# Transposed adjacency parts made beside attention, column sums by matmul, and row statistics made in the last head

## The reference

```python
def _L0_gnn_ref(x, spatial_encoding, edge_encoding, Wq, Wk, Wv, Wout):
    ...
    q = (x @ Wq).reshape(h, n, d)
    k = (x @ Wk).reshape(h, n, d)
    v = (x @ Wv).reshape(h, n, d)
    a = jnp.einsum('hnd,hmd->hnm', q, k) * scale
    a = a + spatial_encoding + edge_encoding
    mask = spatial_encoding == 0.0
    a = jnp.where(mask, -1000000.0, a)
    a = jax.nn.softmax(a, axis=-1)
    a = jnp.where(mask, 0.0, a)
    out = jnp.einsum('hnm,hmd->hnd', a, v)
    out = out.transpose(1, 0, 2).reshape(n, h * d)
    return out @ Wout
def _L1_gnn_ref(X, S, W1, W2, W3, U1, U2, U3, gamma, beta):
    ...
    Rf = S / jnp.clip(S.sum(axis=1, keepdims=True), 1e-12)
    Rb = S / jnp.clip(S.sum(axis=0), 1e-12)[:, None]
    for s in range(STEPS):
        A = _adj_from_feats(Xa, W1, W2, W3)
        Xf = Rf @ Xf
        Xb = Rb @ Xb
        Xa = A @ Xa
        ...
h = jnp.maximum(_layernorm(x, axis=-1), 0.0)
x = x + _L0_gnn_ref(h, adj, adj, L0_gnn_Wq, L0_gnn_Wk, L0_gnn_Wv, L0_gnn_Wout)
h = jnp.maximum(_layernorm(x, axis=-1), 0.0)
x = x + _L1_gnn_ref(h, adj, L1_gnn_W1, ...)
```

## Time and profile before

| | us |
|---|---|
| median of 3 runs | 3375.74 (3369.71 to 3376.3) |
| the profiled execution | 3375.48 |
| its span, first to last instruction | 3373.6 |
| PE busy | 2892.8 (86%) |
| DVE busy | 2192.1 (65%) |
| ACT busy | 1342.0 (40%) |

### The profile page before, as it was taken

The page is one execution under the profiler, slowest core; times in us unless marked ns, Lnnn a source line. Parts: engine busy times, 40 slices in busy tenths (PEclk is TensorE's granted clock), DMA queues, the critical chain, the costliest instruction groups (busy, mean ns, idle before and its releaser), DMA issues. The chain is left out here.

```text
span 3373.6 us, 55939 instructions
## 1 busy us (share of the span) xinstructions
PE 2892.8 (86%) x20376; PEld 2147.8 (64%) x20376; DVE 2192.1 (65%) x4346; ACT 1342.0 (40%) x1734; POOL 59.8 (2%) x71
## 2 busy tenths in 40 slices
PE   2469999999999999999999778878884669687599
PEld 1356676766767667676676447656553556576488
DVE  7966555565555655556556488788488887895531
ACT  5743434434344343443434322333326364522221
POOL 0000000000000000000000000000000000000110
PEclk7579999999999999999999889998997889899899
DMA  7937848578485784857848413000010010100500
GB/s 288 371 144 178 195 107 199 124 177 196 106 199 124 177 196 105 199 124 177 197 102 210 120 47 98 26 13 26 26 38 26 1 51 2 50 26 1 231 1 26
DMA packets 587856, 396.80 MB, mean 118 GB/s; under 512 B 538563, under 2 KB 553414, under 8 KB 562118
## 3 DMA queue, kind: packets, MB, share of 16 engines
q1 hardware_dynamic: 585990, 382.49, 42.1%
q10 hardware_dynamic: 1728, 12.58, 1.1%
HBM read 223.05 MB, written 37.75 MB: 77 GB/s over the span
## 5 line engine op out<-in xcount | busy, mean ns | idle before, releaser
L773 DVE SCALAR_TENSOR_TENSOR e_lo<-e,e_hi 128x2048 f16<-128x2048 f32 x128 | 293.2, 2291 | 435.3 <-ACT e_hi L688 435.3
L625 PE MATMUL av<-vw_hi,pT_hi 128*128 128x256 f16 x2048 | 559.5, 273 | 8.0 <-DMA pT_lo<-e_lo 8.0
L625 PE MATMUL av<-vw_hi,pT_lo 128*128 128x256 f16 x2048 | 559.4, 273 | 0.0
L625 PE MATMUL av<-vw_lo,pT_hi 128*128 128x256 f16 x2048 | 559.4, 273 | 0.0
L614 PE MATMUL logits<-kT_hi,qT_hi 128*128 128x512 f16 x1024 | 388.6, 379 | 2.8 <-DVE att_small L759 1.9
L614 PE MATMUL logits<-kT_lo,qT_hi 128*128 128x512 f16 x1024 | 388.1, 379 | 0.0
L614 PE MATMUL logits<-kT_hi,qT_lo 128*128 128x512 f16 x1024 | 388.1, 379 | 0.0
L682 ACT ACTIVATE att_small<-att_small,minus 128x1 f32<-128x1 f32 x128 | 37.6, 294 | 784.3 <-DVE att_small L768 784.3
L759 DVE CUSTOM_DVE_ANT_0 e<-logits,bias,att_small 128x1024 f32<-128x1024 f32 x256 | 328.6, 1283 | 0.4 <-issue 0.3
L2000 DVE SCALAR_TENSOR_TENSOR nuc_junk<-nuc_e,nuc_thr 128x2048 bf16<-128x2048 f32 x140 | 323.7, 2348 | 4.3 <-issue 0.4
L683 ACT ACTIVATE e<-e,att_small,sc 128x2048 f32<-128x2048 f32 x128 | 266.2, 2080 | 0.0
(11 more groups left out here) (417 smaller groups left out, 5802.6 us busy)
## 6 DMA issues: line engine op xcount, KB each, us to landing
bias<-bias_scratch SPq DMA_DIRECT2D x130, 1024.0 KB, 4.9
bias_scratch<-adj_bias SPq DMA_DIRECT2D x16, 1024.0 KB, 4.5
adjT_scratch<-adjT SPq DMA_DIRECT2D x16, 1024.0 KB, 5.8
nuc_at_hi<-adjT_scratch SPq DMA_DIRECT2D x32, 512.0 KB, 3.8
nuc_at_lo<-adjT_scratch SPq DMA_DIRECT2D x32, 512.0 KB, 4.6
adjT<-adjT_scratch SPq DMA_DIRECT2D x16, 1024.0 KB, 19.8
adj_rows<-in_adj_dram ACTq DMA_DIRECT2D x12, 1024.0 KB, 6.8
adj_rows<-in_adj_dram SPq DMA_DIRECT2D x4, 1024.0 KB, 14.0
```

What stands on the lines that cost most here:

```text
L625: last = nc.tensor.matmul(AV[par], PT[par][w][:, m, :], VW[x][:, m, :], start=(m == 0 and w == x == 0), stop=(m == T - 1 and w == 1))
L773: nc.vector.scalar_tensor_tensor(out=EL[:, :], in0=E[par][:, :], scalar=P_SCALE, in1=EH[:, :], op0=ALU.mult, op1=ALU.subtract).then_inc(lo ...
```

## The change

**Adjacency.** The stage no longer transposes. It keeps the bias part. The column sums come from TensorE: a column of ones against each tile of rows, 4 f32 matmuls of 512 columns per tile, accumulated over the 16 tiles in PSUM; at the end ScalarE copies the row of sums, 16 small matmuls turn it, and VectorE copies it to `deg`.

**Pieces.** The transposed parts are made in `attend`, in heads 3 to 7, in 64 pieces of 128 rows x 512 columns. Their buffers are the columns of `hT_hi` and `hT_lo` that belong to heads 0 to 3. Slot n is the n-th of the 14 slots per head; in slot n SyncE loads piece n, ScalarE and VectorE make high part and remainder of piece n-1, SyncE issues two DMA transposes of piece n-2, and at the head of the slot four stores of piece n-3 in runs of 128 f16. The loops of heads 3 to 7 are written out.

**Projection banks.** K's eight batches go to eight different PSUM banks (`K_BANKS`) and not to two and then a ring of four. In head 0 ScalarE evicts VW ahead of the first `exp`, and `weight_tops` comes earlier on VectorE.

**Statistics.** `bn_stats` and `bn_aggr` of a row tile follow the last `add` of that tile in head 7; `refresh` reads them.

```diff
 def adjacency(...)
+                pe.wait_ge(ones_here, 1)
+                for n in range(T):
+                    pe.wait_ge(loaded[n % AHEAD], 16 * (n // AHEAD) + 16)
+                    for b in range(N // BANK):
+                        cols = slice(b * BANK, (b + 1) * BANK)
+                        last = nc.tensor.matmul(CS[0:1, cols], ones[:, 0:1], A[n % AHEAD][:, cols], start=n == 0, stop=n == T - 1)
+                    last.then_inc(summed, 1)
...
-                    s.wait_ge(at_stored[q], 16 * turn + 16)
-                    for h in range(2):
-                        s.wait_ge(tposed, 2 * n + h + 1)
-                        nc.scalar.activation(half(AT[q][:, 0, :, :], h), TP[q][:, HALF * h:HALF * (h + 1)], ACT.Copy,
-                                             scale=A_SCALE).then_inc(hi_done, 1)
...
+                        s.wait_ge(summed, AHEAD * i + u + 1)
...
-                            nc.vector.tensor_reduce(col[:, T // 2 * h:T // 2 * (h + 1), ds(n, 1)].rearrange("p m a -> p (m a)"),
-                                                    TP[q][:, HALF * h:HALF * (h + 1)].rearrange("p (m n) -> p m n", n=P), X, ALU.add)
...
 def attend(...)
+                def piece_load(n):
...
+                    if n >= 2:
+                        sp.wait_ge(piece_lo, n - 1)
+                    sp.dma_start(PA[n % 2], piece_rows[tile // 2, tile % 2, part, :, :]).then_inc(piece_here[n % 2], 16)
+                def piece_turns(n):
...
+                    sp.wait_ge(piece_lo, n + 1)
+                    if n:
+                        sp.wait_ge(piece_stored, 64 * n)
+                    for x in range(2):
+                        sp.dma_start_transpose(PX_T[x], PX[x]).then_inc(piece_turned, 16)
+                def piece_stores(n):
...
+                    sp.wait_ge(piece_turned, 32 * n + 32)
+                    for x in range(2):
+                        for q in range(2):
+                            sp.dma_start(piece_out[tile, part % 2, :, x, :, q, part // 2, :],
+                                         PX_T[x][q * HALF:(q + 1) * HALF, :, :]).then_inc(piece_stored, 16)
...
+                def items_and_pieces(h):
+                    for t in range(T):
+                        piece_stores(slots(h, t))
+                        item(T * h + t, (t + 2) % T, t % 2)
+                        piece_turns(slots(h, t))
+                        piece_load(slots(h, t))
...
+                def piece_top(n):
...
+                    s.wait_ge(piece_here[n % 2], 16 * (n // 2) + 16)
+                    if n:
+                        s.wait_ge(piece_turned, 32 * n)
+                    nc.scalar.activation(PX[0].rearrange("p (c r) -> p c r", c=CH), permuted(PA[n % 2]), ACT.Copy,
+                                         scale=A_SCALE).then_inc(piece_hi, 1)
+
+                def items_and_pieces(h):
+                    for t in range(SLOTS):
+                        exp(T * h + t + 2, t % 2)
+                        piece_top(slots(h, t))
...
+                def piece_rest(n):
...
+                    v.wait_ge(piece_hi, n + 1)
+                    nc.vector.scalar_tensor_tensor(out=PX[1].rearrange("p (c r) -> p c r", c=CH), in0=permuted(PA[n % 2]), scalar=A_SCALE,
+                                                   in1=PX[0].rearrange("p (c r) -> p c r", c=CH), op0=ALU.mult, op1=ALU.subtract).then_inc(piece_lo, 1)
...
+                    for t in range(SLOTS):
+                        item(h, t, t % 2, link)
+                        if h == HEADS - 1:
+                            shift(T * h + t, t, t % 2)
+                            statistics(T * h + t, t)
+                        piece_rest(slots(h, t))
```

More of the change, by code:

```diff
@@ L351, in _ @@
             @block.tensor
             def _(pe):
-                with pe.Fori(0, T // AHEAD) as i:
-                    for u in range(AHEAD):
-                        n, q = AHEAD * i + u, u % 2
-                        pe.wait_ge(loaded[u], 16 * i + 16)
-                        rows_u = permuted(A[u][:, :])
-                        for h in range(2):
-                            pe.wait_ge(lo_done, 2 * n + h + 1)
-                            for t in range(T // 2 * h, T // 2 * (h + 1)):
-                                last = nc.tensor.transpose(TP[q][:, t * P:(t + 1) * P], rows_u[:, t // 2, t % 2 * P:(t % 2 + 1) * P], ident[:, :])
-                            last.then_inc(tposed, 1)
@@ L367, in _ @@
+                pe.wait_ge(row_here, 1)
+                for t in range(T):
+                    last = nc.tensor.matmul(CT[:, t:t + 1], permuted(col[0:1, :])[:, t // 2, t % 2 * P:(t % 2 + 1) * P], ones[0:1, 0:1],
+                                            start=True, stop=True)
+                last.then_inc(turned, 1)
             @block.scalar
@@ L886, in _, with turn_of_heads @@
                 tops_apart()
-                with v.Fori(0, HEADS - 1) as h:
-                    link = items(h)
+                def turn_of_heads(h, link):
                     weights(h + 1)
@@ L902, in _ @@
                     masks(2, 0, link)
-                link = items(HEADS - 1, ends=True)
+                with v.Fori(0, FIRST_HEAD) as h:
+                    turn_of_heads(h, items(h))
+                for h in range(FIRST_HEAD, HEADS - 1):
+                    turn_of_heads(h, items_and_pieces(h))
+                link = items_and_pieces(HEADS - 1)
                 lo(T * HEADS - 1, 1, link)
@@ L1323, in refresh @@
         with block:
-            if norm:
+            if norm is not None:
                 @block.sync
@@ L1406, in _ @@
                 for b in range(QUADS + 2):
-                    if norm and b < QUADS:
+                    if norm is not None and b < QUADS:
                         s.wait_ge(centred, b + 1)
```

222 lines of the change are left out of this document (132 added, 90 removed).

## The result

| | us |
|---|---|
| before, median of 4 runs | 3372.72 (3365.39 to 3376.3) |
| after, median of 4 runs | 3785.53 (3780.88 to 3790.46) |
| ratio | 1.1226, 95% interval 1.1204 to 1.1248 |
| profiled span, before and after | 3373.6 and 3783.9, +410.3 |
| mean granted TensorE clock, before and after | 0.936 and 0.907 |

The changed kernel is 12.3% slower. The forecast was slower, 3665, in a range of 3470 to 3785: the direction and the place are right, the size is 120 us short, and the median lies just outside the range.

The account below looks back on a forecast made before the run. With pieces, SyncE's in-order queue was taken to bound attention. From 3375.5 us: adjacency -57, small parts -4, -3 and -0.5, attention +354 (+342 slots, +18 turns of heads, -6 catching up) gave 3665, range 3470 to 3785.

Parts of the forecast that it names:

- part 3: Attention, heads 3 to 7: the next `e_hi` waits for a closed path through SyncE's in-order queue; sum 16.3, taken as 16.2 us.
- Part 1: Adjacency stage, 141 us before: less work on VectorE and ScalarE, 16 MB less DMA; about -57 us, bounds -47 to -61.
- The floors of DMA and ScalarE: Adjacency stage: DMA done at 141 us at the earliest, ScalarE's floor at 138.
- DMA loses 16 MB of 46 ... 141 at the earliest: Adjacency stage: the remaining 29.4 MB at 372 GB/s take 79 us from about 62, so 141 at the earliest.
- Part 2: Attention loop: a piece's copy on ScalarE and remainder on VectorE lengthen the item from 10.53 to 12.4 us.
- the transpose behind the bias: SyncE's queue: the transpose of `e_hi` waits for the bias (lands 4.9 after issue), then needs 2.4 more; 7.0 us.
- Slots: Attention, heads 3 to 7: 60 slots pay the longer period, 60 x (16.2 - 10.5) = +342 us.
- The four turns of heads: Attention: ScalarE and VectorE come some 5.7 us later to K's first evictions; +4.5 us each, +18.
- Part 4: Small changes: K over eight banks -4 us, VW evicted before `exp` in head 0 -3, statistics moved -0.5.
- The statistics: Moved from the refresh's start into the last head: -0.5 us in the refresh, 0 in the head, 10 at the most.
- C: Rival: piece stores cost 0.93 us each on SyncE, period 18.1, time 3792; chance 0.08 given for it and D.
- D: Rival: TensorE's clock falls to 1.2 GHz in attention, bursts of 20.8 us bind, 3930; chance 0.08 given with C.

## Why the prediction was right or wrong

The mechanism of the forecast was right and its size was short. The step that failed is the sum in part 3, the closed path through SyncE: 16.3 us added up, 18.6 measured. Of the 120.8 us between forecast and measured change, attention has 115.1 (+462.1 where parts 2 to 4 gave +347), the adjacency stage 13.3 and the refresh 1.3; the nucleus takes 9.3 back, and the rest is 0.4.

**Part 1, -57, measured -43.7**, outside the bounds given (-47 to -61). The floors of DMA and ScalarE were about right, but they weren't what bound. The step that failed is "DMA loses 16 MB of 46 ... 141 at the earliest": the stores of the bias land 7.4 us after their issue (the page's median), there are two bias buffers, and VectorE waited for them 9 times, a term that the sum didn't have. With four the stage ends within 3 us of the forecast.

**Part 2, 12.4.** Measured alone 12.2 to 12.5, but by two errors that cancel. The remainder takes 1.08, the upper bound given ("up to 1.1 if the permuted read costs extra"), not 0.69; and the items of heads 3 to 7, written out, take 10.1 without a piece, not 10.53. The high part took 1.10 as said.

**Part 3, 16.2, measured 18.6.** The path was right in each of its steps and in their order. Term by term, forecast and mean of 54 slots of the changed kernel:

| | forecast | measured |
|---|---|---|
| high part with its hand-over | 1.2 | 1.04 |
| remainder with its hand-over | 0.8 | 1.10 |
| turns, from issue to the first store | 3.1 | 3.74 |
| four stores | 1.8 | 2.64 |
| bias | 0.33 | 0.77 |
| transpose of `e_hi`, to the next `e_hi` | 7.15 | 7.41 |
| `e_hi` | 1.91 | 1.91 |
| sum | 16.3 | 18.6 |

So the terms that were mis-sized are the stores (+0.8), the turns (+0.6), the bias (+0.4), the remainder (+0.3) and the transpose (+0.3). In the slot shown above the bias took 1.12, since SyncE stood 0.5 us ahead of the transpose there, in most slots 0.1; the transpose is 0.4 shorter there. The issue of a plain transfer takes 0.57 to 0.65 here, not 0.33 or 0.45: I took both from the cheap rows. The dearest guess, the transpose behind the bias, came out in part by luck: the bias lands 6.2 us after its issue and not 4.9, the transpose 1.9 after that and not 2.4, and it is issued 0.4 us later behind the bias than I had it. That it waits for the bias to land was right; that the reason is its place in the queue was not, as the bias on GpSimd's queue showed.

**Slots.** 60 forecast, 60 found: 56 of 18.6 and 4 of 15.2. 56 x (18.6 - 10.55) + 4 x 4.7 = +470, where 60 x 5.7 gave +342. The four turns of heads cost +1.6 each at most, not +4.5, and most items without a piece in heads 3 to 7 ran at 10.1. The four turns alone were 13 us too dear in the forecast, against slots 128 us too cheap.

**Part 4.** Turns of heads 1 and 2 -1.0 each, head 0 -3.7, near what was said (-4 and -3). The statistics gave nothing that shows (the refresh took 0.8 us more), as said; the first power of the refresh starts 7.1 us after the stage's first instruction on VectorE (2331.80), as it did before (1913.37 and 1920.44):

```profile
2338.91 4.00 POOL L1448 TENSOR_TENSOR qk_rstd<-qk_rstd,halfp 128x4 f32<-128x4 f32 x4 [2145.11 <-issue]
```

The Trainium skill (GPSIMD Engine Reference, Instruction dispatch) gives some 6 us for loading the code at the first call of a newly loaded kernel. The gap agrees with it and is a little longer, and it stayed although the statistics were there long before; that it is such a load no run here isolates.

**Rivals.** C's number (18.1, 3792) nearly came out, by luck and not by its mechanism alone: the stores' issues were 0.65, not 0.93, and a store landed 2.2 us after its issue. The Trainium skill (DMA: Bandwidth & Descriptors, Specifications) says that writes below 512 bytes become a read and a write. Stores of 64 KB in such runs land in 2.2 us, those of 128 KB in 2.6, so nothing of it shows in a landing. The granted clock fell to 0.83 in paying slots, and TensorE still idled: D didn't come. The rest, by which the total is smaller than attention's +462: the first step of the nucleus took 9.3 us less. The same code ran there in 449 to 461 us from kernel to kernel, with TensorE's granted clock at 0.66 in one stretch before, and 1.00 in the same place after, where 77 matmuls and not 42 fit into about the same busy time:

```profile
2310.00:2330.00 20.00, 15.31 (x42) 7.85 (x41) 18.34 (x46) 4.94 (x11) 0.20 (x1) 0.66 0.00 0
```

```profile
2729.00:2749.00 20.00, 14.86 (x77) 9.44 (x78) 18.19 (x48) 7.92 (x16) 0.00 (x0) 1.00 0.00 1
```

The 9.3 us lie within that spread, so I count them as not belonging to the change; why the clock differs there wasn't tested.

**Range.** Its upper end, 3785, lay 7 us under C, which raised the stores alone, and the median passed it by half a us. With the terms of the path each at its upper bound at once (remainder, turns, stores) it would have held the result (19.9 us, 60 x 9.4 = 564); small errors of one sign along a closed path of seven steps add up, sixty times.

## What to carry to other kernels

Work is only beside other work if its whole path is: here a piece's queue work and its transfers cost more than its arithmetic. Where a single buffer waits for a transfer to land, add up everything that its issuing engine does and waits for in one period, with an issue at the price of the dear rows, and ask which large load it will be issued right behind. Moving that load only moves the payer, from one transpose to the other and then to the stores; and test changes of order together, since those that help alone can cost together. When a change of order shortens a path through several engines, add up the issuing engine's own round as well, landings that it waits for included: it is the next floor.

## What the runs showed of the hardware that was not expected

- A DMA transpose issued up to 1 us behind a 1 MB load keeps SyncE in its issue until about the landing of that load: in the changed kernel 4.9 to 5.6 us, up to 0.2 us before the landing, and it lands itself 1.9 us after the load, 6.9 to 7.9 after its own start. Behind no such load its issue takes 1.5 to 3.6 in the runs with one queue and its median landing is 4.3 to 4.8. It is the same when the load comes from GpSimd's queue (0.1 before, 2.0 after). A plain 64 KB store right behind the load lands with it too (5.0 after its issue, otherwise 2.2; the run with the bias behind both transposes).
- With permuted columns a 128x512 f32 read from SBUF takes VectorE 1.08 us for the remainder and ScalarE 1.10 for the high part, where 0.69 and 0.60 were the rows for plain reads from PSUM. PSUM is hardly the reason: from SBUF, ScalarE's plain `e_hi` takes 1.91 for 2048 columns where the permuted copy takes 3.96, and VectorE's plain `e_lo` 2.29, a quarter of which is 0.57.
- The same items run 0.4 us faster each when the loops on three engines are written out.
- The DMA share can pass 1 (1.14 over 100 us), so it is no measure of what is left.
